# A decoder on one Trainium2 core: a buffer's blank fill in 24 pieces, and two heads to a strip in the late attention sums

## The reference, cut to what matters

```
x = ln(x + taylor_attention(x))               # layer 0
x = ln(x + cross_attention(x, ctx))           # "wide": 16 heads of 64, 77 context rows
x = ln(x + experts_top2(x))                   # gelu, 8 experts
x = ln(x + causal_alibi_attention(x))         # layer 1, "causal": 16 heads of 8, 128 keys
x = ln(x + rope_rmsnorm_cross_attention(x, ctx))  # "rotary": 16 heads of 8, 77 context rows
x = ln(x + experts_top2(x) + shared_mlp(x))   # silu, 8 experts
# each softmax attention, per head:
attn = softmax(q @ k.T * scale (+ bias)); out = attn @ v
```

## Time and profile before

| what | us |
|---|---|
| median of three runs | 2891.46 |
| the profiled execution, its own time | 2890.11 |
| its span, first to last instruction | 2888.3 |
| wide pairs, first z to last | 293 to 998 |
| causal pairs, first z to last | 1421 to 1924 |
| rotary pairs, first z to last | 1992 to 2510 |

### The profile page before, as it was taken

How to read it: one execution, slowest core, us unless ns; L and a number is a source line. 1 busy time by engine, 2 the same in 40 slices (tenths; PEclk the granted TensorE clock), 3 DMA queues, 4 the chain that set the end, 5 groups by cost and what they waited for, 6 DMA issues and landing times. The chain is left out here.

```text
span 2888.3 us, 63045 instructions
## 1 busy us (share of the span) xinstructions
PE 2554.6 (88%) x19424; PEld 1891.0 (65%) x19424; DVE 1952.0 (68%) x5426; ACT 1830.7 (63%) x5343; POOL 1441.1 (50%) x1852
## 2 busy tenths in 40 slices
PE   8998979799798639997899999968999999779996
PEld 6666757578576539995455555546766666547994
DVE  6884757677577635556688888876677777434655
ACT  6773646566465324444799999957888888622334
POOL 4442324445455445554333333326678888723775
PEclk9998989999899869999899999989999999889998
DMA  9923464745747222224010000000000000011336
GB/s 264 338 75 97 153 204 153 245 144 155 241 138 231 86 66 72 71 69 132 12 58 9 11 9 11 9 25 7 17 26 28 29 28 21 26 33 42 92 93 190
DMA packets 274488, 267.96 MB, mean 93 GB/s; under 512 B 29740, under 2 KB 253241, under 8 KB 273776
## 3 DMA queue, kind: packets, MB, share of 16 engines
q1 hardware_dynamic: 256592, 228.42, 26.1%
q0 software_dynamic: 17280, 34.13, 3.5%
q10 hardware_dynamic: 288, 1.38, 0.1%
HBM read 101.24 MB, written 151.85 MB: 88 GB/s over the span
## 5 line engine op out<-in xcount | busy, mean ns | idle before, releaser
L758 POOL TENSOR_TENSOR wide_probs<-wide_exps,wide_inv_sum 128x616 f32<-128x616 f32 x128 | 168.3, 1315 | 385.8 <-DVE wide_inv_sum L1538 299.9
L1248 ACT ACTIVATE causal_exps<-causal_biased,causal_neg_max 128x128 f32<-128x128 f32 x1024 | 325.8, 391 | 31.1 <-DVE causal_neg_max L1552 29.6
L739 POOL DMA_INDIRECT sorted_x<-send,place_i x240 | 244.8, 1020 | 91.7 <-issue 34.9
L1248 ACT ACTIVATE rotary_exps<-banks,rotary_neg_max 128x77 f32<-128x77 f32 x1024 | 251.9, 351 | 15.1 <-DVE rotary_neg_max L1552 14.7
L1050 PE MATMUL banks<-wide_folded,wide_probsT 128*128 128x128 f32 x1280 | 191.1, 281 | 78.1 <-issue 71.7
L1050 PEld LDWEIGHTS banks<-wide_folded,wide_probsT 128*128 128x128 f32 x1280 | 172.0, 197 | 80.4 <-issue 77.6
L1799 ACT ACTIVATE gelu_hidden<-banks,gelu_slot 128x256 f32<-128x256 f32 x284 | 116.7, 471 | 157.1 <-PE banks L1976 157.1
L1499 DVE TENSOR_TENSOR causal_biased<-banks,regions 128x512 f32<-128x512 f32 x256 | 164.6, 685 | 72.2 <-PE banks L1074 69.8
L1730 POOL DMA_INDIRECT results<-gelu_tile_out,gelu_dest_i x142 | 140.2, 987 | 142.4 <-DVE gelu_tile_out L1886 120.1
L1552 DVE TENSOR_REDUCE rotary_neg_max<-banks 128x4 f32<-128x308 f32 x256 | 121.6, 475 | 119.4 <-PE banks L1088 114.6
L1730 POOL DMA_INDIRECT results<-swiglu_tile_out,swiglu_dest_i x142 | 144.2, 1015 | 115.8 <-DVE swiglu_tile_out L1881 60.6
(11 more groups left out here) (384 smaller groups left out, 7214.5 us busy)
## 6 DMA issues: line engine op xcount, KB each, us to landing
v_dram<-wide_staged SPq DMA_DIRECT2D x38, 1024.0 KB, 4.9
sorted_x<-blank SPq DMA_DIRECT2D x1, 34848.0 KB, 116.8
sorted_x<-blank SPq DMA_DIRECT2D x4, 8712.0 KB, 30.6
wide_folded<-v_dram SPq DMA_DIRECT2D x128, 256.0 KB
gelu_tile_in<-sorted_x SPq DMA_DIRECT2D x71, 132.0 KB, 2.1
swiglu_tile_in<-sorted_x SPq DMA_DIRECT2D x71, 132.0 KB, 2.1
gelu_back<-results SPq DMA_DIRECT2D x16, 512.0 KB, 8.0
swiglu_back<-results SPq DMA_DIRECT2D x16, 512.0 KB, 6.0
```

Of the source, the lines that this page charges most:

```text
L739: pool.indirect_dma_start(route["sorted_x"], bass.IndirectOffsetOnAxis(ap=r_place_i[:, b % 2, which, n // 2:n // 2 + 1], axis=0), send[:, ...
L758: pool.tensor_tensor(probs[:, half % SLOTS, 0:HH * NK].rearrange("p (k h) -> p h k", h=HH), exps[:, half % EB], inv_sum[:, half % SLOTS].u ...
L1248: last = act.activation(exps[:, (NU * c.c + k) % ES, h], scores[:, h * NK:(h + 1) * NK], ACT.Exp, bias=neg_max[:, k % SLOTS, h:h + 1])
```

## The change

**The fill.** `FILLS` goes from 4 to 24. The fill leaves `load(f)` and becomes `blank_part(n)`, called after `values_step(pair)` for the pairs 4 to 27, one piece each. Its semaphore counts 24 transfers instead of 4.

**The late sums.** The values get another layout: four groups (sequence, parity) of 8 strips of 32 columns, each group 272 columns long. The strip of an even head starts at its values; that of an odd head starts 16 columns ahead of them, so that its values stand in columns 16 to 24 of the weights. An even unit starts the accumulation in a strip's 32 rows, the odd unit behind it adds to it. A sequence's 16 heads now fill 256 columns of `o_bank[b]`, evicted once (k = 7 and k = 3), and are turned by two transposes. In rotary the order of head groups becomes the one that causal has.

```diff
-FILLS = 4
+FILLS = 24
...
-            values = sb("values", [P, 2, 2, H, STRIP])
+            values = sb("values", [P, 2, STRIPS])
-            sums = sb("sums", [P, 2, NC * P])
+            sums = sb("sums", [P, 2, 2 * P])
...
+        def value_heads(s):
+            return values[:, s].rearrange("p (g r) -> p g r", g=4)[:, :, 0:256].rearrange("p g (x d) -> p g x d", x=8)
         def first_head(j):
-            return 8 * (j % 2) + 4 * (j // 2) if kind == "causal" else HU * j
+            return 8 * (j % 2) + 4 * (j // 2) if late else HU * j
...
+            def blank_part(n):
+                rows, cleared, blank = fill
+                size = SORTED_ROWS // P // 2 // FILLS
+                sp.dma_start(rows.rearrange("(p j k) d -> p j (k d)", p=P, k=2)[:, size * n:size * (n + 1)],
+                             blank.unsqueeze(1).to_broadcast([P, size, 2 * ROW])).then_inc(cleared, 16)
             def step(f, ahead=None, pair=None):
                 if f is not None:
                     load(f)
                 if kind == "wide" and pair is not None:
                     values_step(pair.c)
+                    if 4 <= pair.c < 4 + FILLS:
+                        blank_part(pair.c - 4)
             def load(f):
...
-                if fill is not None and f.c % (n_pairs // FILLS) == n_pairs // FILLS - 1:
-                    rows, cleared, blank = fill
...
-                pool.memset(values[:, :, :, :, D:D + 1], 1.0).then_inc(ready, 1)
+                for s in range(2):
+                    last = pool.memset(value_heads(s)[:, :, :, D:D + 1], 1.0)
+                last.then_inc(ready, 1)
...
             def turn_back(u, b):
-                pe.wait_ge(o_done, u.count(OG, 2 * b + 2))
+                pe.wait_ge(o_done, u.count(2, b + 1))
...
-                for n in range(NC):
-                    at = first_head(n) * STRIP
-                    last = pe.transpose(f_bank[:, at:at + P], sums[:, b, n * P:(n + 1) * P], ident)
+                for n in range(2):
+                    last = pe.transpose(f_bank[:, n * P:(n + 1) * P], sums[:, b, n * P:(n + 1) * P], ident)
...
+            def late_sum(pair, n):
+                b, j = divmod(n, UB)
+                g, odd = divmod(j, 2)
+                pe.wait_ge(probsT_done, pair.count(NU, n + 1))
+                if n == 0:
+                    pe.wait_ge(front_done, pair.count(FU, FU))
+                if j == 0 and pair.back(1).real:
+                    pe.wait_ge(o_done, pair.back(1).count(2, b + 1))
+                for h in range(HU):
+                    strip = 272 * 2 * b + 256 * odd + 32 * (4 * g + h)
+                    last = pe.matmul(o_bank[b][32 * h:32 * h + 32, g * P:(g + 1) * P], values[0:NK, pair.c % 2, strip:strip + 32],
+                                     probsT[0:NK, n % 2, h * P:(h + 1) * P], start=odd == 0, stop=odd == 1)
+                last.then_inc(pv_done, 1)
...
-                    if kind == "rotary" and at is not None and at[1] % 2 == 1:
+                    if kind == "rotary" and at is not None and at[1] % UB == UB - 1:
...
-                        act.activation(sums[:, b, j * P:(j + 2) * P], o_bank[(m // 2) % 2][:, 0:2 * P], ACT.Copy).then_inc(o_done, 1)
+                        act.activation(sums[:, b], o_bank[b][:, 0:2 * P], ACT.Copy).then_inc(o_done, 1)
...
-                by_head = f_bank.rearrange("p (h d) -> p h d", h=H)
+                by_head = f_bank[:, 0:2 * P].rearrange("p (x odd d) -> p x odd d", odd=2, d=16)
```

More of the change, by code:

```diff
@@ L436, in softmax_attention @@
         xT = sb("xT", [P, 2, 2, P])
-        if kind != "wide":
-            values = sb("values", [P, 2, 2, H, STRIP])
+        if late:
+            values = sb("values", [P, 2, STRIPS])
         keys = sb("keys", [P, 2, H, 2, NK] if kind == "wide" else [P, 2, KH, NK])
@@ L691, in make_keys @@
             b, j = divmod(piece, KH // HU)
-            heads = slice(HU * j, HU * (j + 1))
+            at = HU * j if kind == "causal" else first_head(j)
+            heads = slice(at, at + HU)
             mask = heads8[:] if kind == "causal" else consts["heads16"]
@@ L860, in front_act @@
                     return act.activation(qT[:, s2], two, ACT.Identity, bias=q_bias[:], scale=8.0 ** -0.5)
-                return act.activation(values[:, s2, :, :, 0:D], f_bank[:, 0:2 * P].rearrange("p (b h d) -> p b h d", b=2, h=H), copy)
+                return act.activation(value_heads(s2)[:, :, :, 0:D], f_bank[:, 0:2 * P].rearrange("p (g x d) -> p g x d", g=4, x=8), copy)
             if m == 1:
@@ L866, in front_act @@
             if m == 3:
-                return act.activation(values[0:NK, s2, :, :, 0:D],
-                                      f_bank[0:NK, 0:2 * P].rearrange("p (b h d) -> p b h d", b=2, h=H), copy)
+                return act.activation(value_heads(s2)[0:NK, :, :, 0:D], f_bank[0:NK, 0:2 * P].rearrange("p (g x d) -> p g x d", g=4, x=8), copy)
             if f.back(2).real:
@@ L1086, in step @@
                                 q = qT[:, c.c % 2, b]
-                                moving = keys[:, b, HU * j:HU * j + HU]
+                                moving = keys[:, b, first_head(j):first_head(j) + HU]
                             pe.matmul(s_bank[k % 2][:, 0:HU * NK], q, moving, start=True, stop=True).then_inc(s_ps, 1)
@@ L1110, in step @@
                     if at is not None and late:
[L1111 to L1125, removed]
+                        late_sum(*at)
                     if f is not None:
@@ L1507, in divide @@
                     dve.wait_ge(oT_ps, u.back(1).count(2, b + 1))
-                dve.tensor_tensor(o[:, b], by_head[:, :, 0:D], inv_total[:, b].unsqueeze(2).to_broadcast([P, H, D]), ALU.mult).then_inc(norm_done, 1)
+                dve.tensor_tensor(o[:, b].rearrange("p (odd x) d -> p x odd d", odd=2), by_head[:, :, :, 0:D],
+                                  by_pair.unsqueeze(3).to_broadcast([P, H // 2, 2, D]), ALU.mult).then_inc(norm_done, 1)
             def step(e, roots, f, c, u, n, r=None, *later):
@@ L1561, in step @@
                     at = lagged(c, u, k, OLAG)
[L1562 to L1565, removed]
+                    if kind == "causal" and at is not None and at[1] % UB == UB - 1:
+                        pair, b = at[0], at[1] // UB
+                        dve.wait_ge(pv_done, pair.count(NU, at[1] + 1))
                         if pair.back(1).real:
                             dve.wait_ge(back_ps, pair.back(1).count(2, b + 1))
-                        dve.tensor_copy(sums[:, b, j * P:(j + 2) * P], o_bank[(m // 2) % 2][:, 0:2 * P]).then_inc(o_done, 1)
+                        dve.tensor_copy(sums[:, b], o_bank[b][:, 0:2 * P]).then_inc(o_done, 1)
                     if f is not None and kind == "wide":
```

13 lines of the change are left out of this document (5 added, 8 removed).

## The result

The changed kernel takes 2796.15 us, the median of four runs (2791.9 to 2803.23), against 2891.84 us for the kernel before (four runs, 2889.1 to 2892.94). The ratio is 0.9673, 95% interval 0.9651 to 0.9695. The forecast was 2795, the range 2780 to 2821. The profiled execution's own time is 2791.9 us, its span 2789.1; the forecast for the profiled execution was 2794.

The account below looks back on a forecast made before the run. TensorE was taken to pace the wide and rotary stages, with four fills stalling the wide one. -77.6 (fill) - 0 (causal) - 19 (rotary) + 0.5 (zero fill) = -96.1 us, from median 2891.46 to 2795; range 2780 to 2821.

Parts of the forecast that it names:

- 77.6: Wide stage: gain in us from removing the four fills' stalls, 25 pairs at 20.58 us against 592.05 us.
- The free stretch of 8 to 10 us: Wide stage: idle time of SP's queue in every pair, claimed to hide a piece costing 5.1 us.
- 5.1: Wide stage: estimated us of SP's queue that one piece of 1452 KB takes, 30.6 / 6.
- The third rival: Wide stage: a piece delays the fullest pairs' folded rows, 15 us left, or rotary gain falls to 8; 2806 to 2821, chance 0.17.
- the slower case: Wide stage: each of 24 pieces makes store and folded rows late by 5.1 us; 2918 us, chance 0.03.
- between those two chains ScalarE works without a gap: Causal stage: no removed eviction or transpose lies in ScalarE's two wait chains, so the gain is 0 us.
- The TensorE term: Rotary stage: TensorE has no idle time, so fewer transposes save 0.44 us a pair, 14.1 us over 32 pairs.
- ScalarE's term: Rotary stage: an eviction ahead of the router's matmul goes, saving half of its 10.2 us wait, 5 us.
- ScalarE stood ahead of TensorE: Rotary stage: rival that ScalarE is the pacer, its removed evictions counting in full, 27 for 19; 2787 us, chance 0.1.
- Zero fill and slower starts: Both late stages' starts: zero fill of 2176 columns for 2048 and one more small fill, +0.5 us together.
- half of causal's 30 us: Causal stage: rival that lighter VectorE and TensorE shift the loop, gaining half of 30 us; 2780 us, chance 0.08.
- the signs of being right: All stages: no wide pair over 22 us, causal pairs 16.60, rotary pairs near 15.7 before sending and 16.7 after.

Follow-up runs that it names:

- experiment 4: The kernel of experiment 3 with causal evictions cut to 128 columns: only at k = 5, 2802.53 us (16.46 a pair); only the three others, 2812.2 us (16.60).
- experiment 2: The changed kernel with the two dropped transposes per sequence put back, as copies into unused columns: 2811.94 us.
- experiment 3: The changed kernel with four evictions of 256 columns a pair again (128 columns read twice), transposes still halved: 2805.62 us.
- sums-alone run: The changed kernel with the fill as before, four pieces of 8712 KB among the loads: 2878.45 us, ratio 0.9953 to the kernel before.

## Why the prediction held, and where it did not

**The fill: held.** 78.6 us for 77.6, and the 20 more transfers cost nothing that shows. The queue's free time hides the piece, as forecast, though not for quite the reason given. The free stretch of 8 to 10 us was read from the emptier of the two pairs; in the fuller one leave 6 to 8. A piece lands in 8.5 us and not in 5.1, but 12.9 and 17.1 us for two and three times its size make some 4.3 us for each further 1452 KB, so that as a price of the queue's time 5.1 was near. Its place behind the folded loads, on which the prediction relied, makes no difference, and twice the piece is hidden as well. The third rival (a piece delays the folded rows of the fullest pairs) and the slower case have fallen: no store's issue takes over 2.1 us, no pair is over 21.6. A stall in proportion to the bytes is refuted by the 12 pieces; that a stall does come with larger ones is shown by the 8.

**Causal: the step "between those two chains ScalarE works without a gap", so 0 us, failed; it measured 4.8.** VectorE adds slopes four times a pair, and the prediction looked at the two times with idle time ahead of them. Ahead of the fourth, for units 6 and 7, stands the eviction at k = 5. ScalarE had no gap there, but it had lost an overlap. The timeline of before, ahead of the exponentials of unit 6:

```profile
1613.18 0.41 DVE L1568 COPY causal_sums<-banks 128x256 f32<-128x256 f32 x1
...
1613.51 1.27 DVE L1499 TENSOR_TENSOR causal_biased<-banks,regions 128x512 f32<-128x512 f32 x2
1613.61 1.27 ACT L1248 ACTIVATE causal_exps<-causal_biased,causal_neg_max 128x128 f32<-128x128 f32 x4
...
1614.70 0.67 DVE L1552 TENSOR_REDUCE causal_neg_max<-causal_biased 128x4 f32<-128x512 f32 x1
1614.79 0.58 ACT L1232 ACTIVATE causal_probsT<-banks 128x512 f32<-128x512 f32 x1
...
1615.41 1.28 ACT L1248 ACTIVATE causal_exps<-causal_biased,causal_neg_max 128x128 f32<-128x128 f32 x4
```

The eviction at 1613.18 holds the slopes to 1613.51, the maxima end at 1614.70 + 0.67 = 1615.37, and the exponentials start at 1615.41, 1.80 us behind those of unit 5. The same place after:

```profile
1531.36 0.68 DVE L1561 TENSOR_REDUCE causal_neg_max<-causal_biased 128x4 f32<-128x512 f32 x1
...
1531.98 1.29 DVE L1506 TENSOR_TENSOR causal_biased<-banks,regions 128x512 f32<-128x512 f32 x2
...
1532.39 1.27 ACT L1256 ACTIVATE causal_exps<-causal_biased,causal_neg_max 128x128 f32<-128x128 f32 x4
...
1533.18 0.68 DVE L1561 TENSOR_REDUCE causal_neg_max<-causal_biased 128x4 f32<-128x512 f32 x1
...
1533.56 0.58 ACT L1240 ACTIVATE causal_probsT<-banks 128x512 f32<-128x512 f32 x1
...
1534.04 1.27 ACT L1256 ACTIVATE causal_exps<-causal_biased,causal_neg_max 128x128 f32<-128x128 f32 x4
```

The slopes follow the maxima at once, the maxima are there at 1533.18 + 0.68 = 1533.86, and the exponentials start at 1534.04, 1.65 us behind the ones before: 0.15 of the 0.16. In the kernel before ScalarE's copy of the probabilities ended at 1615.37 too (1614.79 + 0.58), so the exponentials seemed to wait for nothing but their own engine. In the kernel after they start 0.10 us before that copy ends (1533.56 + 0.58 = 1534.14). The profile shows no idle time in the kernel before; the delay shows only in the distance between the exponentials. Of the 0.41 us that the eviction takes ahead of the slopes, 0.16 counted, and experiment 4 shows that it is the eviction at this place. To stand ahead of slopes is not enough: the eviction at k = 1 does too (1605.38, the slopes at 1605.87), and a shorter one there does nothing. What the transposes have to do with half of the 0.16 (16.52 in experiment 2) stays open: that run brings back four transposes and not the eviction.

**Rotary: the mechanism held, two sizes were off.** 15.8 us for 19. The TensorE term, 0.44 us a pair, is right to the hundredth in the pairs before sending (16.13 to 15.70, experiment 2), but it was taken for all 32 pairs. In the 20 pairs with sending, transposes are worth 0.17, 3.4 us where the sum has 0.44 x 20 = 8.8. ScalarE's term (5 us, half of the router's wait) was too small there: the evictions are worth 0.33 x 20 = 6.6 us, with the reservation made in experiment 3. The wait itself, at line 992 now, fell by more than the half assumed: over the whole stage from 10.7 us (10.2 in the stretch of the earlier trace rows) to 3.3. The waits of the stage (us, times, longest):

```profile
ACT rotary_probsT L1240 <- PE banks L1121: 29.5, 87, 1.5
...
PE banks L845 <- DVE rotary_o L1516: 9.5, 9, 1.2
...
PE banks L992 <- ACT regions L1192: 3.3, 10, 0.4
```

The transposes of the scaled queries and keys (845) wait 9.5 us, where they waited 7.5 before. In these pairs TensorE has waits of its own; that an instruction less is partly only more waiting there fits this and is not shown. ScalarE's wait for the transposes hardly moved (33.0 to 29.5 over the stage), so its lighter load did not become waiting. By the Trainium skill, "Perfetto Trace Analysis", section Identifying the Most-Contended Engine, weight loads are a better measure of how near TensorE is to its limit than matmul time. By that ScalarE stood ahead of TensorE (58.36 to 47.25 us in the earlier trace rows); experiments 2 and 3 show the opposite for the pairs before sending, and a mixture for the others.

**Zero fill and slower starts:** +0.5 us, as summed, but not as reasoned. The zero fill grew by the 0.11 us of the sum at either start (1.81 to 1.92 us, 1.96 to 2.06), yet causal starts as early as before and rotary 0.5 us later. Where the rest of rotary's 0.5 comes from is not shown; that the sum came out is luck.

**The accumulation,** taken as equal, is: the late sums take 285 ns a matmul, as before.

**The total and the range.** That the median comes within 1.2 us of the forecast is in part luck: causal's 4.8 us were not forecast, 3.2 of rotary's were missing, and the four runs lie between 2791.9 and 2803.23. The range took its upper end from a rival that did not come, its lower from half of causal's 30 us, of which 4.8 came. Of the signs of being right two failed: causal pairs are 16.44 us and not 16.60, rotary pairs with sending 16.90 and not 16.7.

## What to carry to other kernels

A large transfer is cheap or dear by what queues behind it: find how much of each pair's time the queue moves nothing, and cut the transfer so that a piece fits. Cutting further gained nothing here (12 or 24 pieces), and one step too few (8) brought half of the stall back, 37 of 79 us, in part through a wait that the large transfer did not have. An engine that shows no idle gap can still be waiting: compare the distance between two instructions of one kind (1.65 against 1.80 us here) along the loop, and if one is longer without a reason, look at what stands ahead of its operands on the other engines. The price of an instruction on the bounding engine holds for the stretch in which that engine is without waits, not for the whole stage.

## What the runs showed of the hardware that was not expected

**A short VectorE operation can last as long as GpSimd's work.** In the sums-alone run GpSimd starts on the rotary keys, VectorE's 128x64 addition 0.09 us later:

```profile
2283.27 1.36 POOL L701 TENSOR_TENSOR rotary_keys<-rotary_kT,rest 128x308 f32<-128x308 f32 x2
...
2283.36 2.39 DVE L1408 TENSOR_TENSOR rotary_r_prefix<-rotary_r_prefix 128x64 f32<-128x64 f32 x1
...
2284.59 1.07 POOL L799 TENSOR_TENSOR rotary_scaled<-rotary_rotated,rotary_qk_rstd 128x512 f32<-128x512 f32 x1
...
2287.76 0.71 PE L1048 MATMUL banks<-wo_plain,rotary_oT 128*128 128x128 f32 x4 [1.88 <-ACT rotary_oT L1197]
```

```profile
2290.00:2292.00 2.00, 2.00 (x16) 1.39 (x15) 1.47 (x8) 0.89 (x3) 0.92 (x2) 0.50 0.42 105
```

The addition takes 2.39 us and ends at 2285.75, just after GpSimd's second operation does (2284.59 + 1.07 = 2285.66). In the changed kernel the same addition, 0.10 us behind the same GpSimd work, takes 0.70:

```profile
2270.99 1.36 POOL L702 TENSOR_TENSOR rotary_keys<-rotary_kT,rest 128x308 f32<-128x308 f32 x2
...
2271.09 0.70 DVE L1409 TENSOR_TENSOR rotary_r_prefix<-rotary_r_prefix 128x64 f32<-128x64 f32 x1
...
2273.81 0.71 PE L1049 MATMUL banks<-wo_plain,rotary_oT 128*128 128x128 f32 x4 [0.21 <-ACT rotary_oT L1198]
```

There it ends at 2271.79, 0.09 us behind the end of the first of GpSimd's two operations in the row (2270.99 + 0.71 = 2271.70). In the sums-alone run the 1.7 us pass to the maxima, ScalarE and TensorE, which stands 1.88 us ahead of the output projection instead of 0.21; then the clock falls to 0.50 (1.2 GHz; the windows row from 2290), and the next pair is 2.5 us longer as well. Three such additions follow one another in a pair. In the kernel before, the second of them takes 1.75 us in each of the four cycles of pairs, where it takes 0.21 in the changed kernel, and there too it ends 0.08 us behind a GpSimd operation (2225.37 + 1.75 = 2227.12, behind 2227.04). The Trainium skill, "SBUF — State Buffer", section SBUF: two separate sides, says that VectorE and GpSimd share a pair of ports as an exclusive lock: a VectorE operation with two inputs in SBUF, as this addition has, and a GpSimd operation that reads SBUF exclude each other, and who starts first holds the ports for the whole instruction. The rows agree that the addition ends where a GpSimd operation does. They show besides that it can stand through the changes from one GpSimd operation to the next: three in a row in the sums-alone run. What decides between 0.70 and 2.39 is not shown; the two runs differ by 0.01 us in the start of the addition behind GpSimd's. The run with the transposes back has three such pairs (19.8 us), and the kernel with the piece ahead of the store and the one with 8 pieces have one each (20.15 and 20.16), all with this addition at 2.39 or 2.40 us. Whether the slower three of the changed kernel's four runs have such pairs isn't shown, as only the fastest has a trace.

**Some causal pairs lose clock in two of the kernels.** In experiment 3, causal, with two transposes in place of four and the pair still at 16.60 us, five pairs take 18.17 us, and five in the run with the three short evictions (there is none in the run with the short one at k = 5). The pair behind a long one takes 16.38, so each costs some 1.35 us. The windows of an ordinary pair, of the long one behind it, and of 4 us in that:

```profile
1455.08:1471.68 16.60, 15.20 (x134) 8.30 (x133) 14.40 (x33) 15.29 (x46) 5.63 (x7) 1.00 0.03 9
1471.68:1489.85 18.17, 16.77 (x134) 8.85 (x133) 14.46 (x32) 16.03 (x49) 5.64 (x7) 0.91 0.03 9
1485.00:1489.00 4.00, 3.92 (x19) 1.78 (x19) 1.81 (x3) 2.49 (x8) 0.00 (x0) 0.57 0.01 2
```

The clock is 0.57 over 4 us: it falls from 1.00 (2.4 GHz) to 0.50 (1.2 GHz) from 1486 to 1488. Before it TensorE had waited 1.05 us at the second turned output; but so it had in the ordinary pair, and in the kernel before, without a fall:

```profile
1468.48 0.30 PE L1045 MATMUL banks<-first,causal_o 128*128 128x128 f32 x1 [1.05 <-ACT causal_oT L1199]
...
1485.08 0.30 PE L1045 MATMUL banks<-first,causal_o 128*128 128x128 f32 x1 [1.05 <-ACT causal_oT L1199]
```

```profile
1600.39 0.30 PE L1022 MATMUL banks<-first,causal_o 128*128 128x128 f32 x1 [1.05 <-ACT causal_oT L1190]
```

In the kernel before and with the transposes back causal's clock is 1.00 throughout the stage, with that wait at 1.05 and 0.97 us. The changed kernel, at 16.44 us a pair, keeps 1.00. What makes the difference, between the kernels or from pair to pair, was not tried and is not shown.
